# Nucleus scores of a graph layer: two products a chunk over a stacked query, instead of three

## What is computed

```python
def _adj_from_feats(Xa, W1, W2, W3):
    Q = Xa @ W1
    K = Xa @ W3
    logits = Q @ W2 @ K.T / TAU
    ...
    keep = jnp.take_along_axis(keep_sorted, inv, axis=1)
    masked = jnp.where(keep, logits, -jnp.inf)
    return jax.nn.softmax(masked, axis=1)
...
for s in range(STEPS):
    A = _adj_from_feats(Xa, W1, W2, W3)
    Xf = Rf @ Xf
    Xb = Rb @ Xb
    Xa = A @ Xa
    Z = Z + (Xf @ U1[s] + Xb @ U2[s] + Xa @ U3[s])
```

## Time and profile before

| | us |
|---|---|
| median of 3 runs (1233.53 to 1237.58) | 1233.69 |
| the profiled execution's own time | 1233.21 |
| its span | 1231.1 |
| PE busy | 945.5 (77%) |
| DVE busy | 782.9 (64%) |
| ACT busy | 481.9 (39%) |
| POOL busy | 111.4 (9%) |

### The profile page before, as it was taken

The page is one execution under the profiler, slowest core; times in us unless marked ns, Lnnn a source line. Parts: engine busy times, 40 slices in busy tenths (PEclk is TensorE's granted clock), DMA queues, the critical chain, the costliest instruction groups (busy, mean ns, idle before and its releaser), DMA issues.

```text
span 1231.1 us, 14056 instructions
## 1 busy us (share of the span) xinstructions
PE 945.5 (77%) x4873; PEld 782.7 (64%) x4873; DVE 782.9 (64%) x1286; ACT 481.9 (39%) x864; POOL 111.4 (9%) x123
## 2 busy tenths in 40 slices
PE   3998899786997979976797049897970599855874
PEld 3788788685997969965586038775430355544763
DVE  4653545542665437874699943235899964959993
ACT  4104655262332422227588112234888411211112
POOL 0000000001453014430400000001000000000000
PEclk9999999987999889998999569999995799997897
DMA  8000000000000000002043000002120010000001
GB/s 330 18 1 4 18 1 1 0 1 1 1 0 18 1 1 1 0 4 54 1 124 87 0 1 1 17 19 63 48 70 0 22 49 24 1 1 1 0 0 46
DMA packets 41808, 31.64 MB, mean 26 GB/s; under 512 B 3154, under 2 KB 39708, under 8 KB 41756
## 3 DMA queue, kind: packets, MB, share of 16 engines
q1 hardware_dynamic: 41756, 30.97, 8.2%
HBM read 29.58 MB, written 1.39 MB: 25 GB/s over the span
## 4 chain that ended last, share of the span: by engine, by line
PE 22%; DVE 13%; issue 13%; ACT 6%; ACTq 0%; DVEq 0%; POOL 0%
PE out L773 5%; ACT u_rows_a L589 3%; PE turned_ps L907 3%; PE scores L889 3%; DVE e_strip L1467 2%; PE scores L804 2%; PE turned_ps L889 2%; DVE small L1252 2%; DVE run L1353 1%; DVE e_strip L1470 1%; DVE e_rows L1473 1%; PE out L898 1%; PE scores L814 1%; DVE tmp L1344 1%; PE scores L683 1%
## 5 line engine op out<-in xcount | busy, mean ns | idle before, releaser
L589 ACT ACTIVATE u_rows_a<-e_rows,small 128x1354 f32<-128x1354 f32 x104 | 146.5, 1411 | 20.0 <-DVE small L1291 20.0
L773 PE MATMUL out<-h_rows,adj_strip 128*128 128x256 f32 x484 | 110.8, 386 | 0.0
L744 PE MATMUL out<-feat,adj_t 128*128 128x256 f32 (+1 forms) x484 | 109.2, 384 | 1.5 <-DVE x_rows L1072 1.5
L744 PEld LDWEIGHTS out<-feat,adj_t 128*128 128x128 f32 x484 | 92.5, 191 | 16.1 <-DVE x_rows L1072 1.9
L773 PEld LDWEIGHTS out<-h_rows,adj_strip 128*128 128x128 f32 x484 | 93.1, 196 | 12.2
L1297 DVE SCALAR_TENSOR_TENSOR tmp<-e_rows,small 128x1354 f32<-128x1354 f32 x52 | 84.5, 1624 | 0.0
L375 POOL TENSOR_TENSOR strip_lo_buf<-tmp,strip_hi_buf 128x1408 fp32r<-128x1408 f32 x22 | 71.5, 3250 | 119.6 <-ACT strip_hi_buf L476 114.4
L483 ACT ACTIVATE y_rows<-scores,small 128x1354 f32<-128x1354 f32 x22 | 30.7, 1394 | 131.5 <-DVE small L1209 131.4
L889 PE MATMUL scores<-feat_fb,adj_strip 128*128 128x512 f32 x154 | 70.7, 617 | 3.5 <-ACT e_rows L575 3.5
L673 PE MATMUL turned_ps<-ident,tmp 128*128 128x128 f32 x132 | 29.3, 318 | 54.8 <-ACT tmp L424 39.8
L1297 DVE SCALAR_TENSOR_TENSOR kept_tile<-e_rows,small 128x1354 f32<-128x1354 f32 x39 | 63.4, 1626 | 0.0
(11 more groups left out here) (326 smaller groups left out, 2270.2 us busy)
## 6 DMA issues: line engine op xcount, KB each, us to landing
adj_strip<-in_adjT SPq DMA_DIRECT2D x22, 704.0 KB, 4.7
adj_t<-in_adjT SPq DMA_DIRECT2D x11, 704.0 KB, 12.6
x_rows<-in_x SPq DMA_DIRECT2D x2, 512.0 KB, 4.2
tmp<-in_L_gnn_W_stack SPq DMA_DIRECT2D x2, 512.0 KB, 4.0
u_weights<-in_L_gnn_U SPq DMA_DIRECT2D x4, 256.0 KB, 3.5
out_rows<-y_rows SPq DMA_DIRECT2D x2, 512.0 KB
tmp<-in_L_gnn_U SPq DMA_DIRECT2D x2, 256.0 KB, 2.9
x_rows<-in_x SPq DMA_DIRECT2D x1, 384.0 KB, 6.7
```

The lines of the kernel that those rows point to most:

```text
L589: act.activation(out2[:, (k % 2) * N:(k % 2 + 1) * N], E[:, t, :], [ACT.Relu, ACT.Sign][k % 2], bias=nudged[:, t:t + 1], accum_out=[relu_s ...
L744: ins = pe.matmul(bank[:, 0:n], AT[:, j, cols(t)], features[:, j, 0:n], start=(j == 0), stop=(j == NT - 1))
L773: ins = pe.matmul(OUT[b][:, 0:D], ADJ[:, b, j, :], H[:, j, :], start=(j == 0), stop=(j == NT - 1))
```

## The change

The high and the low part of a query are put over each other in one operand `aq_hi_lo` (AQ): partitions 0 to 63 hold the high part, 64 to 127 the low part. For that the projection's weights hold W1 times W2 twice and W3 twice, in place of the zeros, so that the features stand in both halves of `qk_t_hi` and `qk_t_lo`. One product over 128 partitions then gives high times high plus low times high, and a second one over partitions 0 to 63 alone gives high query times low key. `aq_hold` only takes up the freed space, so that all else stays where it was.

```diff
-            AQH = sb("aq_hi", [P, 2, P], F32R, scope)
-            AQL = sb("aq_lo", [P, 2, P], F32R, scope)
+            AQ = sb("aq_hi_lo", [P, 2, P], F32R, scope)
+            sb("aq_hold", [P, 2, P], F32, scope)
...
             def q_a(s0):
-                return stage_q(s0, 1, TQH, TQL, lambda b: AQH[:, b:b + 1, :], lambda b: AQL[:, b:b + 1, :])
+
+                def step(t, b):
+                    wait(pool, scored, s0 + t - 1)
+                    pool.tensor_copy(AQ[0:64, b:b + 1, :], TQH[0:64, 0:1, cols(t)])
+                    pool.tensor_copy(AQ[64:P, b:b + 1, :], TQL[64:P, 0:1, cols(t)]).then_inc(q_staged, 1)
+                return step
...
                 pipeline(pool, (0, q_a(SCO[name])))
+                pool.wait_ge(q_staged, SCO[name] + NT)
                 if name == "A0":
...
+                    pool.wait_ge(x_beta, 1)
...
                     for c, n in CHUNKS:
-                        for m, (q, k2) in enumerate([(AQH, TQH), (AQL, TQH), (AQH, TQL)]):
-                            ins = pe.matmul([SC, TP][b][:, c:c + n], q[:, b, :], k2[:, 1, c:c + n], start=(m == 0),
-                                            stop=(m == 2))
+                        pe.matmul([SC, TP][b][:, c:c + n], AQ[:, b, :], TQH[:, 1, c:c + n], start=True, stop=False)
+                        ins = pe.matmul([SC, TP][b][:, c:c + n], AQ[0:64, b, :], TQL[0:64, 1, c:c + n], start=False,
+                                        stop=True)
                     ins.then_inc(scored, 1)
...
             dve.tensor_copy(raw[:, :, 0:64], W12[:, :, :])
-            dve.memset(raw[:, :, 64:128], 0.0)
-            dve.memset(raw[:, :, 192:256], 0.0).then_inc(raw_ready, 1)
+            dve.tensor_copy(raw[:, :, 64:128], W12[:, :, :])
+            dve.tensor_copy(raw[:, :, 192:256], raw[:, :, 128:192]).then_inc(raw_ready, 1)
```

## The result

The changed kernel takes 1261.97 us (median of 4 runs, 1259.32 to 1265.07), the kernel before 1233.66 beside it (4 runs, 1233.53 to 1237.58). The ratio is 1.0225, 95% interval 1.0198 to 1.0252: slower by 2.2%, against 1260 predicted, in a range of 1229 to 1272.

What follows compares the result with a forecast made beforehand. It took a loop of PE, DVE and ACT, none at its peak, to bound stages A0 and A1. 1233.2 + 27.2 (heights and lower clock) + 0.1 (small things) = 1260.5, given as 1260 us, range 1229 to 1272.

Steps and rivals of the forecast that it cites:

- What bounds the kernel now: Stages A0 and A1: a PE, DVE, ACT loop, about 5.6 us an even tile, six tiles making a 33.0 us stage.
- Three products fewer, 0.61 us an even tile: Scoring on PE: dropping two 512-column products and one of 330 saves 0.61 us an even tile, 7.3 us in all.
- A change of height, 0.20 us, in both directions: Between 128- and 64-partition products on PE: five changes cost 1.0 us a tile; net of savings, +4.7 us over 12 tiles.
- The split: One change of height on PE: the weight load waits about 0.15 us, then lies open for about 0.10.
- A long product may cover it: Reason given for the lower bound of 0 us on a change of height; the upper bound was 0.26.
- The lower clock: PE in A0 and A1 falls to 1.2 GHz; a tile takes 4.4 us, 13.6 us lost a stage, 27.2 in both.
- The bounds of the slow stage: Loss in A0 and A1 at the lower clock: 7.6 to 20 us a stage, together 15 to 40.
- Why the clock falls: PE in A0 and A1: a third fewer columns in a longer tile, with an empty array between products.
- Small things: Two DVE memsets become copies, 0.1 us in all; POOL's copies stay 0.29 us each and its added waits cost nothing.
- The rivals: Other cases: free heights, full clock 0.12 or partly low 0.12; heights alone 0.14; one direction 0.10; rest 0.02.
- The free change at full clock: Rival: changes of height in A0 and A1 are hidden under long products and the clock holds, 1226.5 us; chance 0.12.
- Free with a partly low clock: Rival: changes of height are free but the clock falls in four of twelve even tiles, 1231 us; chance 0.12.

Runs made afterwards that it cites:

- kernel 9: Kernel before with two of the nine products of a tile over 64 partitions, four changes of height a tile: 1240.20 us, ratio 1.0047.
- kernel 7: Changed kernel with all products over 128 partitions, plus one unread 512-column product behind each tile: 1228.02 us, ratio 0.9952.
- kernel 11: Changed kernel with all products over 128 partitions, plus two unread 512-column products behind each tile: 1226.11 us, ratio 0.9927.
- kernel 6: Kernel before with the last 16 columns of each third product as a separate product over 64 partitions: 1282.57 us, ratio 1.0409.
- kernel 1: Changed kernel with the second product of each chunk over all 128 partitions, so one height throughout: 1232.50 us, ratio 0.9964.
- kernel 8: Changed kernel plus three unread 512-column products over 128 partitions behind each tile: 1286.49 us, ratio 1.0436.
- kernel 5: Kernel before with one of the nine products of a tile over 64 partitions, two changes of height a tile: 1236.46 us, ratio 1.0021.
- kernel 3: Kernel before with all nine products of a tile over 64 partitions, no change of height: 1248.93 us, ratio 1.0116.
- kernel 2: Changed kernel with the same six products reordered, three over 128 partitions, then three over 64: 1239.67 us, ratio 1.0040.
- kernel 10: Changed kernel with products grouped by height, plus three unread full-height products behind each tile: 1234.07 us, ratio 0.9992.
- kernel 4: Kernel before with the third product of each chunk over 64 partitions, six changes of height a tile: 1283.78 us, ratio 1.0394.

## Why the prediction was right

The time (1262 against 1260) and the mechanism hold: heights cost, the clock falls, PE becomes the bound. That the sum came out within 0.1 us a stage is luck, as the terms of the lower clock show. Step by step:

- *What bounds the kernel now.* Right. In kernel 9 the 0.60 us added to each even tile show up as 3.55 a stage, six times one tile; and DVE and ACT kept their durations throughout.
- *Three products fewer, 0.61 us an even tile.* Right: kernels 7 and 11 take 33.0 - 29.4 = 3.6 us off A0, 6 x 0.61 = 3.7.
- *A change of height, 0.20 us, in both directions.* Right in size and in both directions (0.40 to 0.43 us between all starts of 512 columns). The Trainium skill's page TensorEngine Tiling (Array Packing), section Key Properties, by which a change of tiling mode drains the engine, agrees with the trace: loads start only with their own product. The split was read less well: 0.15 and 0.10 from the earlier trace rows, 0.1 and 0.1 in kernel 6. The 0.20 itself was a choice inside bounds of 0 and 0.26, from one row. "A long product may cover it", the reason for the lower bound, is refuted: 512 columns cover nothing.
- *The lower clock.* Right that it falls and stays; the terms were off and made up for each other. The change was scaled to 0.35 by the ratio of two loads, the median of the earlier trace rows and their longest, 1.76; it measured 0.72 - 0.43 = 0.29, and the loads of the changed kernel take 0.28 at the lower clock where they took 0.19, 1.5 times. A tile is 4.03 us, not 4.4, and a pair 8.07, not 8.8. A pair took 5.49 before (577.55 to 605.00 is five), so 2.6 is lost a pair and not 3.2. On the other side only the first tile of a stage ran at the full clock, where the prediction let the first pair and the next even tile through, and the last tile, with no odd one beside it, loses 2.0 (7.58 us from its first product to the stage's end, 5.56 before), where the prediction counted it as a whole pair. From the starts of the products A0 adds up to 1.1 for the first pair (6.63 against 5.49), 4 x 2.6 and 2.0: 13.5, where 0.8 + 4 x 3.2 = 13.6 was predicted.
- *The bounds of the slow stage.* The upper one is added up wrong: changes at 0.26 x 1.76 make a tile of 5.0 us and a pair of 10.1, and five pairs then lose 22 us and not 20. The range would have reached some 5 us higher; nothing measured comes near it.
- *Why the clock falls.* Two causes stood in one sentence, a third fewer columns and an empty array between products. The first makes only dips (kernel 1). Six gaps a tile suffice with nearly all the work there (kernels 6 and 8), two and four do not (kernels 5 and 9), and a cause that the prediction didn't have, half height, suffices without gaps (kernel 3). The changed kernel has both, and taking one away doesn't bring its clock back: not with the changes grouped (kernel 2), and not with full-height work beside them (kernel 8). Six gaps also make the tile longer, so the same work is spread over more time; these runs don't separate the gap from that.
- *Small things.* Right, and the 0.1 was nothing: on DVE L1243 starts at 551.56 and the operation behind the three copies at 551.97, 0.41 us, where one copy and two memsets took 0.42 before (552.55 to 552.97).

```profile
551.56 0.23 DVE L1243 COPY tmp<-w 128x128 f32<-128x128 f32 x1
551.70 0.22 DVE L1244 COPY tmp<-w 128x128 f32<-128x128 f32 x1
551.84 0.22 DVE L1245 COPY tmp<-tmp 128x128 f32<-128x128 f32 x1
551.97 0.83 DVE L1001 BATCH_NORM_AGGREGATE mean_var<-stats 128x2 f32<-128x6 f32 x11
```

- *The rivals.* The free change at full clock, 1226.5, is what kernels 7 and 11 do once the change of height is taken away (0.9952 and 0.9927 of 1233.7 are 1227.8 and 1224.7). Free with a partly low clock, 1231, is kernel 1 (0.9964: 1229.3). They were well sized, for a kernel that wasn't this one.

Left open: what exactly the chip measures when it sets the clock, and why A1 has a dip in kernels 5, 7, 10 and 11 where A0 of the same kernels has none while its tiles run. Each of these dips begins in the first 1.5 us of A1, when PE is still at the first tile or at the extra products right behind it, so what PE did before the stage has a part in it. PE rests 2.40 to 2.56 us in front of A1 and 1.89 to 1.98 in front of A0; but it rests 2.40 there in the kernel before and in kernel 9 too, whose clocks hold, so the rest alone doesn't decide it. Whether moving between two groups of 64 partitions, without a change of height, costs anything was not tried.

## What to carry to other kernels

Leaving out zero rows saves nothing in a product: 512 columns take 0.23 us over 64 partitions (kernel 3) as over 128. It puts 0.20 us (0.29 at the lower clock) between the product and a neighbour of another height, and it may cost the clock. So fill the height with something harmless (here low times low) and keep one height through a stage, or at least group the heights; where PE is then so idle that the clock dips, a product that nothing reads, placed where PE waits anyway, can pay for itself (kernels 7 and 11). Judge such a change by start-to-start times and the granted clock, not by PE's busy time or the number of products.

## What was not expected of the hardware

- The granted clock goes with the height of the products as well: nine products a tile at 0.23 us each hold it at 1.00 over 128 partitions and lose it over 64 (kernel 3), although the other 64 held zeros.
- A full queue of products doesn't bring the clock back if the heights alternate: in kernel 8 PE had work in front of it for 59 us and the clock was 0.52; the same nine products in kernel 10's order had 0.99 in A0 and 0.79 in A1.
- One product of nine, with its two changes of height, decides it: with two over 64 partitions a tile (kernel 9) the clock is 1.00 and 1.00, with three (kernel 4) 0.52 and 0.51, 1240 against 1284 us.
